# The first sequence of a two-block transformer kernel on one core: one VectorE step per ternary weight tile, fc1 a tile ahead, weight joins moved

## What is computed

```
block 0 (all matmuls quantized: rows of activations to int8, weights to -1, 0, 1)
  weight_quant(w): s = 1/mean|w|;  wq = clip(round(w*s), -1, 1)/s
  xn  = rmsnorm(x)*(1+scale) + shift          scale, shift from the condition
  qkv = act_quant(xn) @ weight_quant(w_qkv).T ; 16 heads of 32, softmax
  x  += act_quant(o)  @ weight_quant(w_proj).T
  h   = gelu(act_quant(xn2) @ weight_quant(w_fc1).T)
  x  += act_quant(h)  @ weight_quant(w_fc2).T
block 1 (float32): one head of 512, softmax(h Q K' h' / sqrt(512)), V and proj,
  then h = gelu(h @ mlp_w1) @ mlp_w2, both with a residual
```

## Time and profile before

| | |
|---|---|
| three executions | 2284.70, 2288.89, 2292.79 us, median 2288.89 |
| profiled execution | 2284.53 us, its span 2282.7 us |
| busy in the span | TensorE 2029.6, VectorE 1581.3, ScalarE 1149.2, GpSimd 722.1 us |
| first product of block 1 (L1368) | starts at 357.71 us |
| mean granted TensorE clock | 0.958 of full speed |

### The profile page before, as it was taken

How to read it: one execution, slowest core, us unless ns; L and a number is a source line. 1 busy time by engine, 2 the same in 40 slices (tenths; PEclk the granted TensorE clock), 3 DMA queues, 4 the chain that set the end, 5 groups by cost and what they waited for, 6 DMA issues and landing times.

```text
span 2282.7 us, 40192 instructions
## 1 busy us (share of the span) xinstructions
PE 2029.6 (89%) x13491; PEld 1019.2 (45%) x13491; DVE 1581.3 (69%) x2821; ACT 1149.2 (50%) x2082; POOL 722.1 (32%) x661
## 2 busy tenths in 40 slices
PE   3867787989998999899988999899989999899889
PEld 3345333444444444444445444444445444444434
DVE  5678636887578756886588757886588757885422
ACT  4365544564448444555447444655457443754230
POOL 1153233442126402541135302622145212731121
PEclk8788898999999999899999999999999999999989
DMA  6632452212230213111230213121230223011212
GB/s 225 207 103 100 159 187 88 86 39 84 88 103 25 102 60 126 48 57 65 94 106 18 101 71 125 39 84 56 85 112 20 86 91 116 25 57 56 93 37 92
DMA packets 85523, 200.82 MB, mean 88 GB/s; under 512 B 7612, under 2 KB 48864, under 8 KB 73144
## 3 DMA queue, kind: packets, MB, share of 16 engines
q1 hardware_dynamic: 74920, 166.49, 21.7%
q10 hardware_dynamic: 10384, 31.49, 3.8%
HBM read 161.97 MB, written 35.72 MB: 87 GB/s over the span
## 4 chain that ended last, share of the span: by engine, by line
PE 55%; issue 17%; DVE 14%; ACT 7%; POOL 5%; DMA 1%; DVEq 0%; ACTq 0%; POOLq 0%; SPq 0%
PE banks L1368 11%; PE banks L1370 10%; PE banks L1369 10%; PE banks L1326 5%; PE banks L1261 4%; POOL memory L1193 3%; DVE memory L1144 3%; PE banks L1138 2%; PE banks L1047 2%; DVE memory L961 2%; PE banks L1208 2%; PE banks L1182 2%; PE banks L1243 1%; PE banks L1312 1%; DVE memory L976 1%
## 5 line engine op out<-in xcount | busy, mean ns | idle before, releaser
L1368 PE MATMUL banks<-memory 128*128 128x512 bf16 x1536 | 589.5, 384 | 32.3 <-DVE memory L1616 11.8
L1369 PE MATMUL banks<-memory 128*128 128x512 bf16 x1536 | 584.7, 381 | 0.0
L1370 PE MATMUL banks<-memory 128*128 128x512 bf16 x1536 | 584.6, 381 | 0.0
L1193 POOL TENSOR_TENSOR memory<-memory 128x512 bf16<-128x512 f32 x288 | 324.4, 1146 | 317.3 <-ACT memory L1189 316.0
L1144 DVE TENSOR_REDUCE memory<-banks 128x1 f32<-128x512 f32 x512 | 333.6, 680 | 47.0 <-PE banks L1138 44.4
L1189 ACT ACTIVATE memory<-banks 128x512 f32<-128x512 f32 x512 | 290.3, 596 | 138.9 <-PE banks L1182 137.6
L1594 POOL TENSOR_TENSOR memory<-memory 128x512 bf16<-128x512 f32 x128 | 144.6, 1132 | 583.3 <-DVE memory L1589 583.3
L1368 PEld LDWEIGHTS banks<-memory 128*128 128x128 bf16 x1536 | 149.3, 97 | 220.2 <-DVE memory L1616 19.3
L1138 PE MATMUL banks<-memory 96*128 96x512 bf16 x512 | 198.5, 411 | 52.9 <-DVE memory L1144 46.9
L1370 PEld LDWEIGHTS banks<-memory 128*128 128x128 bf16 x1536 | 148.9, 97 | 187.5 <-issue 5.6
L1369 PEld LDWEIGHTS banks<-memory 128*128 128x128 bf16 x1536 | 152.3, 99 | 165.6 <-issue 5.0
(11 more groups left out here) (175 smaller groups left out, 2880.3 us busy)
## 6 DMA issues: line engine op xcount, KB each, us to landing
memory<-weight_parts SPq DMA_DIRECT2D x80, 1024.0 KB, 4.9
memory<-head_parts SPq DMA_DIRECT2D x192, 128.0 KB, 2.8
head_parts<-memory SPq DMA_DIRECT2D x64, 256.0 KB, 2.8
weight_parts<-memory ACTq DMA_DIRECT2D x10, 1024.0 KB, 4.9
...
memory<-in_L_cond_w_fc ACTq DMA_DIRECT2D x2, 4096.0 KB, 14.2
...
```

The source lines that it names most:

```text
L1193: eng.tensor_tensor(prob_lo[:, e % RING], expo[:, e % RING], prob_hi[:, e % RING], ALU.subtract).then_inc(ok.sem, 1)
L1368: pe.matmul(bank, lh, rh, start=(k == 0), stop=False)
L1369: pe.matmul(bank, lh, rl, start=False, stop=False)
L1370: mm = pe.matmul(bank, ll, rh, start=False, stop=(k == KC - 1))
```

## The change

- `ternary` has one VectorE instruction in place of two: times the factor, plus MAGIC. The result may be any whole number. ScalarE reads the banks with `Sign` and a bias of -MAGIC in place of `Identity`, which gives -1, 0 or 1. ScalarE's stream holds six table loads (`ACT_TABLE_LOAD`) before and after.
- In the first sequence `prob_low` goes to GpSimd for 52 tiles and to VectorE for 12: all up to tile 41, and every second one from 42 to 60, are GpSimd's. The loop keeps its lists.
- `LATE_TURNS` moves seven of eight entries two slots or so ahead.
- TensorE's MLP of the first sequence is written apart: fc1 of tile t + 1 stands ahead of fc2 of tile t.
- The joins stand at other places (tables `JOIN_PE`, `JOIN_ACT`, `JOIN_DVE`). `join_small_rows` goes from the middle of the MLP to the place ahead of the turning of its input, `small` and the value bias from the fourth to the second tile, the last product of v and proj from the second tile to behind fc2 of the last; VectorE turns v's weights ahead of the row maxima (`amax0`), not behind the scales.
- The split pieces have four buffers (STAGES), two of them in the space of the turned q and k weights, which must have been read first. Loads and stores are issued by SyncE.

```diff
-LATE_TURNS = ((1, 4), (1, 10), (2, 0), (2, 6), (2, 12), (3, 2), (3, 10), (3, 14))
+LATE_TURNS = ((1, 4), (1, 8), (1, 14), (2, 4), (2, 10), (3, 0), (3, 8), (3, 12))
...
+JOIN_PE = {'proj': ('qk first',), 'gain': ('qk last',), 'turn': ('turn v', 'rows'), 1: ('small', 'bias'), 0: ('vp first',), 4: ('vp last',)}
+JOIN_ACT = {'head': ('qk 0',), 'round': ('qk 1',), 'square': ('qk 2', 'qk 3', 'turn v', 'qk store'), 'turn': ('split 0',), 'copy': ('split 1',), 0: ('split 2', 'vp 0', 'vp 1', 'split 3'), 1: ('split 4',), 2: ('split 5',), 3: ('split 6', 'split 7'), 'norm': ('vp 2', 'vp 3', 'vp store')}
+JOIN_DVE = {'scale': ('qk 0',), 'whole': ('qk 1',), 'add': ('qk 2',), 'gain': ('qk 3',), 'shift': ('turn v',), 'turn': ('rows',), 0: ('vp 0', 'vp 1'), 'norm': ('vp 2', 'vp 3'), 1: ('small', 'bias')}
...
+RAMP_LOW = (42, 44, 46, 48, 50, 52, 54, 56, 58, 60)
+FIRST_POOL = [e for e in range(KC * HEADS) if e < RAMP_LOW[0] or e in RAMP_LOW]
+FIRST_LOW_DVE = [e for e in range(KC * HEADS) if e not in FIRST_POOL]
...
+        stages = [ring[:, n] for n in range(UNITS)]
+        stages += [xy_w[:, n * 2048:(n + 1) * 2048].bitcast(BF16) for n in range(STAGES - UNITS)]
...
         def split_high(act, n):
             act.wait_ge(piece_in[n % 3], 16 * (n // 3 + 1))
-            if n >= UNITS:
-                act.wait_ge(piece_out[n % UNITS], 16 * (n // UNITS))
-            act.activation(ring[:, n % UNITS, 0:KC * D], pieces[n % 3], ACT.Copy
-                           ).then_inc(prep["split_high"], 1)
-            if n > 0:
-                store_piece(act, n - 1)
-                if n + 2 < N_PIECES:
-                    load_piece(act, n + 2)
+            if n >= STAGES:
+                act.wait_ge(piece_out[n % STAGES], 16 * (n // STAGES))
+            elif n >= UNITS:
+                act.wait_ge(prep["join_full"], ROWS + 2)
+            act.activation(stages[n % STAGES][:, 0:KC * D], pieces[n % 3], ACT.Copy).then_inc(prep["split_high"], 1)
...
-                act.activation(dst, banks[:, 6 + job % 2], ACT.Identity, bias=-MAGIC, saturate=False
+                act.activation(dst, banks[:, 6 + job % 2], ACT.Sign, bias=-MAGIC, saturate=False
...
-            chain(dve, dve.tensor_scalar(part, part, inv_w[:, which:which + 1], 1.0, ALU.mult, ALU.min))
-            dve.tensor_scalar(part, part, -1.0, MAGIC, ALU.max, ALU.add).then_inc(prep["ternary"], 1)
+
+            dve.tensor_scalar(part, part, inv_w[:, which:which + 1], MAGIC, ALU.mult, ALU.add
+                              ).then_inc(prep["ternary"], 1)
...
+                if j is None:
+                    done(sp, plan0, ("o", H - 1), i)
+                    for n in range(3):
+                        load_piece(sp, n)
                 if ahead:
...
+                if j is None:
+                    for n in range(N_PIECES):
+                        store_piece(sp, n)
+                        if n + 3 < N_PIECES:
+                            load_piece(sp, n + 3)
...
             for n in range(UNITS):
+                sp.wait_ge(piece_out[n], 16 * N_PIECES // STAGES)
+                sp.wait_ge(joined_out, 16 * (n + 1))
                 load_unit(sp, 0, n)
...
-                for t, (m0, m1, m2, m3) in enumerate(CUTS):
+                if j is None:
+
+                    fc1_0(pe, i, 0)
+                    join(j, 0)
+                    fc1_0(pe, i, 1)
+                    for t in range(1, TT + 1):
+                        turn_hidden(pe, i, t - 1, range(4))
+                        if t + 1 < TT:
+                            fc1_0(pe, i, t + 1)
+                        fc2_0(pe, i, t - 1)
+                        join(j, t)
+                for t, (m0, m1, m2, m3) in enumerate(CUTS if j is not None else ()):
```

174 lines of the change are left out of this document (95 added, 79 removed).

## The result

The changed kernel took 2250.38 us (median of four executions, 2247.48 to 2252.33) beside 2286.97 of the kernel before in the same comparison: a ratio of 0.984, 95% interval 0.9821 to 0.9859. Forecast were 2253 us within 2236 to 2272. The profiled execution took 2250.43 us with a span of 2248.6; the one of before took 2284.53. So the profiles differ by 34.1 us, the medians by 36.6.

The account below looks back on a forecast made before the run. TensorE was taken to bound the loop from 357.7 us on, and the chain of waits the start before it. Savings of 6.3 + 14 + 15.5 = 35.8 us off a 2288.9 median gave 2253 us, range 2236 to 2272.

Parts of the forecast that it names:

- Preparation: Stretch 0 to 116.7 us: ada1's chunks ready sooner, DMA queue passing on that shift; 6.3 us saved, between 4 and 9.
- Attention: Stretch 116.7 to 224 us: shorter waits for ternary step and bank, rests moved to GpSimd; 14 us saved, bounds 0 and 22.
- Joins: Stretch 224 to 262 us, before the MLP: L981 shorter, row product filling TensorE's wait; net 1 us saved, between -3 and 3.
- MLP: Stretch 262 to 357.7 us: fc1 ahead and joins moved; 15.5 us saved including 1 from the joins, bounds 5 and 22.
- tile 0's 2 us for tiny steps: In the MLP's first tile: 2 us added because its tiny steps would stand behind a split on GpSimd.
- The loop: From block 1's first product on: left as it is by the change, 1925 us within 4.
- the case of no change: Whole kernel: the loop loses in clock what the start gains, some 2% of its 1925 us; chance 0.02.
- the shared port: Rival in attention: VectorE and GpSimd block each other on the rests, costing 5 us, 2258 in all; chance 0.18.
- The clock came back: Rival in attention: without long pauses TensorE stays at its upper clock level, 8 us more saved, 2245; chance 0.13.
- The ternary step was the limit after all: Opposite rival: ScalarE's magnitudes or GpSimd take the step's place, attention saves nothing, 2267; chance 0.05.
- the waits did not change hands: Opposite rival in the MLP: splits or a late piece hold ScalarE, only 5 us saved, 2264; chance 0.12.
- Sign asked for no further table load: Opposite rival: Sign in another set than Exp, two table loads per pair of reads, 56 us, 2309; chance 0.02.

Follow-up runs that it names:

- the second execution: The changed kernel run once more with nothing altered, beside the follow-up runs: 2250.24 us, ratio 0.9851 to the kernel before.

## Why the prediction was right, and where its steps were off

The number holds, and the chain came out in kind: the start got shorter and the loop began earlier. Two steps did not hold. One is the sentence that every us off the chain should come off the total: block 1 starts 40.1 us earlier, and the median fell by 33.2 and 36.6 in the two comparisons. The other is that attention was priced by the waits alone, with the clock kept as it was. By its steps, with what the profile of the changed kernel has:

- **Preparation, 6.3 forecast, 8.5 measured** (9.4 in the second execution, 9.7 with the step alone). The 6.1 us for ada1 and the order of the DMA queue were right in kind: the stacking of parts was issued at 102.31 instead of 111.02, and the first scores by key still wait for DMA. The step that was too strict is that the queue passes on only ada1's part: ScalarE issued the load of fc1 at 89.24 instead of 96.69, 7.4 us earlier and not 6.1, and the first scores by query shifted from 75.10 to 68.62. The bound of 9 was crossed in the second execution; the key spreads over 2.4 us with the same code.
- **Attention, 14 forecast, 12.6 and 12.9 measured.** The parts are near: I gave 9.2 + 2.0 to the waits for the step and for the bank, and the step alone brought 10.3; I gave 3 to the rests and nothing to the slots, and the two together brought 2.3 to 2.6, with the short step and with the long one (104.9 against 107.2). But the sum has no term for the clock, and TensorE's idle time fell by 6.0 us, not by 14: ScalarE's reads and sums took the place of part of the waits. The other 6.7 us are the clock, 0.84 to 0.91, which I had left out of the sum and put into the upper bound and a rival. That the two come to nearly 14 together is luck. Putting back the rests alone costs 5.3 to 5.6 and the slots alone 1.9 to 2.1, more than the pair is worth, because the new slots beside the old rests are worse than the old slots.
- **Joins, 1 forecast, 1.9 measured, but not for my reason.** L981's 2.68 us did go (0.17 now), and the row product did fill the wait, but it took 8.73 us, not 7.0, and nothing came out of it. The run with the short step alone, with the joins at their old places, has 36.6 us as well. What changed is the clock at the start of the stretch: with a pause ahead of proj's turn (1.56 us), its product ran at a reduced clock (5.25 us); without one, in 3.61. The first join product is the slower for it, 8.71 us instead of 7.12, but that falls into a wait for VectorE. The run with the old turns, where the first join product takes 7.12 us and proj 5.30 as before, has the 38.0 us of before.
- **MLP, 14.5 forecast, 17.7 measured.** Tile 0 took 11.8 from its hidden step to its whole numbers, not 13.6: its tiny steps did fall beside a split on GpSimd and were not held (rows below). Tile 1 took 12.5 for 13.0, tile 2 16.4 for 15.9, held by the value bias as forecast, tile 3 10.6 for 10.3, and the end 8.2 for 9.0; the first hidden step also followed its fc1 0.9 us sooner than before. So the failed step of this term is tile 0's 2 us for tiny steps; the rest are sizes.
- **The way to block 1, forecast unchanged, measured 17.9 against 17.3.** The norm beside the memset stayed, as I said, and could have gone; I counted it as given.
- **The loop, forecast 1925 within 4, measured 1931.0 and 1927.2.** The bound was too tight: over the 14 profiles it moves by 9 us. And its centre moved: by the medians it is 1931 to 1932 in the changed kernel and 1925 before. I had named this, a loop that loses in clock what the start gains, for the case of no change only, where it takes a seventh of the gain. My own sign of being wrong, "if the loop changes", is met by it in part.

The gains sum to 8.5 + 12.6 + 1.9 + 17.7 - 0.6 = 40.1 us, 4.3 more than the 35.8 of the forecast, and the loop took 6.0 back in the profiled execution. So 2250.4 beside 2253 is better than the steps were: two errors stand against each other, a start that gained 4.3 more and a loop that gave back 6. The 2253 also goes from a median of 2288.9 for the kernel before, where its 44 executions have 2284.6; with that one the same sum gives 2248.8.

Of the rivals, the shared port is real in its mechanism (871 against 697 ns a tile), and the runs put it at 2.1 us where I had 5; it does not decide. The clock came back in attention, 0.84 to 0.91, and that is inside the 12.6: more than half of it, so this rival was the nearest to what happened, though 8 us more did not come. The ternary step was the limit after all (10.3 us of attention by itself), and in the MLP the waits did not change hands, as it saved 17.7. Sign asked for no further table load.
